# A perceiver layer on one core: queries of two tiles projected together, row normalisation moved to ScalarE, and self values moved behind values

## What is computed

```python
q = split_heads(layernorm(x) @ Wq.T + bq)          # 16 heads of 16
k = split_heads(ctx @ Wk.T + bk);  v = split_heads(ctx @ Wv.T + bv)
x = x + merge(softmax(q @ k.T) @ v) @ Wo.T + bo
x = x + self_attention(layernorm(x))               # RMS norm, rotary, sigmoid weights, 32 x 32 per batch
x = x + experts(layernorm(x))                      # 8 experts, top 1, capacity 160
```

## Time and profile before

| | us |
|---|---|
| three runs | 1109.96, 1110.98, 1110.84 (median 1110.84) |
| profiled execution, its own time | 1106.06 |
| its span, first to last instruction | 1104.1 |
| PE busy | 1066.6 (97%) |
| DVE busy | 882.3 (80%) |
| ACT busy | 796.4 (72%) |
| POOL busy | 244.1 (22%) |

### The profile page before, as it was taken

How to read it: one execution, slowest core, us unless ns; L and a number is a source line. 1 busy time by engine, 2 the same in 40 slices (tenths; PEclk the granted TensorE clock), 3 DMA queues, 4 the chain that set the end, 5 groups by cost and what they waited for, 6 DMA issues and landing times.

```text
span 1104.1 us, 40835 instructions
## 1 busy us (share of the span) xinstructions
PE 1066.6 (97%) x16195; PEld 869.6 (79%) x16195; DVE 882.3 (80%) x2652; ACT 796.4 (72%) x2319; POOL 244.1 (22%) x521
## 2 busy tenths in 40 slices
PE   6899999999999999999999999999999999988996
PEld 5678787787888788887787888788888778766996
DVE  6788798898888888888898888888888888874211
ACT  5778687788787787787787787787787787742221
POOL 1011212222222222212222222222222222221112
PEclk9999999999999999999999999999999999999998
DMA  7333422222221222112222221222212221001673
GB/s 202 109 101 102 154 63 67 68 68 64 60 64 44 61 62 57 49 50 60 61 61 61 60 60 42 59 56 56 48 48 58 58 61 36 17 12 47 207 249 110
DMA packets 69260, 82.04 MB, mean 74 GB/s; under 512 B 14331, under 2 KB 48076, under 8 KB 69072
## 3 DMA queue, kind: packets, MB, share of 16 engines
q1 hardware_dynamic: 64896, 75.06, 23.6%
q0 software_dynamic: 3360, 3.72, 1.0%
q10 hardware_dynamic: 816, 0.66, 0.2%
HBM read 64.79 MB, written 16.56 MB: 74 GB/s over the span
## 4 chain that ended last, share of the span: by engine, by line
PE 72%; DVE 18%; issue 4%; DMA 2%; ACT 1%; SPq 1%; POOL 1%; POOLq 0%; DVEq 0%; ACTq 0%
PE kps L416 12%; PE vps L428 12%; PE score L462 9%; PE score L448 5%; PE gather L477 5%; PE shared L486 5%; PE shared L501 4%; DVE prob L1092 4%; DVE nmx L1081 4%; PE score L778 3%; PE score L764 3%; PE shared L527 3%; DVE ctx_p L1073 2%; PE shared L405 2%; DVE th L1175 2%
## 5 line engine op out<-in xcount | busy, mean ns | idle before, releaser
L830 ACT ACTIVATE prob<-score,nmx 128x257 f32<-128x257 f32 x512 | 235.8, 475 | 95.8 <-DVE nmx L1081 95.8
L416 PE MATMUL kps<-ctx_p,wk_p 128*128 128x512 f32 x768 | 217.4, 411 | 0.0
L428 PE MATMUL vps<-wv_p,ctx_p 128*128 128x256 f32 x1536 | 215.5, 290 | 0.0
L1081 DVE TENSOR_REDUCE nmx<-score 128x2 f32<-128x514 f32 x256 | 165.2, 687 | 59.2 <-PE score L448 59.0
L428 PEld LDWEIGHTS vps<-wv_p,ctx_p 128*128 128x128 f32 x1536 | 191.7, 190 | 14.1 <-issue 12.7
L416 PEld LDWEIGHTS kps<-ctx_p,wk_p 128*128 128x128 f32 x768 | 138.1, 190 | 38.5 <-issue 13.6
L1092 DVE TENSOR_SCALAR prob<-prob,rsum 128x256 f32<-128x256 f32 x512 | 159.3, 354 | 9.1
L462 PE MATMUL score<-const,prob 128*128 128x128 f32 x1024 | 153.5, 278 | 5.5 <-DVE prob L1092 3.3
L1558 POOL TENSOR_TENSOR rstd<-ve,const 128x1 f32<-128x1 f32 x64 | 53.2, 831 | 464.6 <-DVE ve L1210 235.7
L462 PEld LDWEIGHTS score<-const,prob 128*128 128x128 f32 x1024 | 114.7, 141 | 16.3 <-DVE prob L1092 14.9
L847 ACT ACTIVATE ctx_p<-ctxT,nlast 128x256 fp32r<-128x256 f32 x256 | 116.0, 511 | 4.2 <-issue 4.2
(11 more groups left out here) (227 smaller groups left out, 1734.7 us busy)
## 6 DMA issues: line engine op xcount, KB each, us to landing
ctxT<-in_ctxT SPq DMA_DIRECT2D x128, 257.0 KB, 3.2
w<-in_w SPq DMA_DIRECT2D x16, 1024.0 KB, 8.1
xq<-in_x SPq DMA_DIRECT2D x32, 128.0 KB, 2.1
xr<-in_x SPq DMA_DIRECT2D x32, 128.0 KB
qbd<-qkT SPq DMA_DIRECT2D x248, 16.0 KB, 1.8
out<-row SPq DMA_DIRECT2D x31, 128.0 KB
slots<-row SPq DMA_DIRECT2D x10, 257.0 KB, 5.1
x_a<-slots SPq DMA_DIRECT2D x8, 129.0 KB, 2.1
```

What stands on the lines that cost most here:

```text
L416: last = mm(kps[:, :], wk_p[:, x, n, c * P:(c + 1) * P], ctx_p[:, y, n, 2 * r:2 * r + 2, :].rearrange("p j s -> p (j s)"), start=(n, x) == ...
L428: last = mm(vps[:, c, :], ctx_p[:, x, n, j, c * P:(c + 1) * P], wv_p[:, y, n, :], start=(n, x) == (0, LO), stop=(n, y) == (C - 1, LO))
L830: last = af(prob[:, m, :], score[:, m, 0:S], ACT.Exp, bias=nmx[:, m:m + 1], scale=1.0, accum_out=esum[:, m:m + 1])
L1081: v.tensor_reduce(nmx[:, 2 * c:2 * c + 2], score[:, 2 * c:2 * c + 2, 0:S], AX.X, ALU.max, negate=True).then_inc(s["max_done"], 1)
```

## The change

Seven edits go together.

1. The queries of tiles 1 to 30 are projected in 15 pairs. `project_pair` runs in every second pass, with fp32r parts of the weight (`wq_p`) and of the rows (`xnT_p`): 12 matmuls of 256 columns in place of twice 4 fp32 matmuls of 128 columns (which the profile counts as twice 8). Tiles 0 and 31 keep the old projection.
2. For the parts, ScalarE copies the high part of the transposed rows (`queries_hi`) and VectorE subtracts it (`queries_lo`, new in the sequence of j = 1). ScalarE's `queries` runs once per pair over 256 columns.
3. `norm_x_apply` moves from VectorE to ScalarE, behind the last copies of j = 3, for the tile three ahead; GpSimd computes the shift that it needs. `norm_x` moves ahead of `maxima(i, 3)`.
4. `sigmoid_product` moves behind `maxima(i, 1)`.
5. In j = 3 `norm2` moves between the two halves of `normalise`, and `context_lo(i + 1, 3)` behind `probsT(i, 3)`.
6. The first half of the self values moves from place (1, 1), ahead of the values, to (1, 2), behind them.
7. GpSimd waits for the normalisation of j = 1 before `rms`, and for that of j = 3 before `residual_bias2`.

In pass 0 the rows of tiles 1 and 2 are both normalised by VectorE and transposed, and SyncE waits for them before it loads the rows of tile 3.

```diff
+            def project_pair(p):
+                pe.wait_ge(s["xnT_parts"], 2 * p + 2)
+                if once(p):
+                    pe.wait_ge(s["wparts_done"], C + 2)
+                for c in range(C):
+                    for n in range(C):
+                        for x, y in PASSES:
+                            last = mm(shared[:, c * 2 * P:(c + 1) * 2 * P], wq_p[:, x, n, c * P:(c + 1) * P],
+                                      xnT_p[:, y, n].rearrange("p w q -> p (w q)"),
+                                      start=(n, x) == (0, LO), stop=(n, y) == (C - 1, LO))
+                last.then_inc(s["q_ps"], 1)
...
-                    (1, 1): s2 and (lambda: self_values(t2, range(0, 8))),
-                    (1, 2): lambda: (s1 and (spare_free(xa, i, 1), transpose_rows(y1, "y1_done", t1, "y1t_ps", spare_c)),
+                    (1, 2): lambda: (s2 and self_values(t2, range(0, 8)),
+                                     s1 and (spare_free(xa, i, 1), transpose_rows(y1, "y1_done", t1, "y1t_ps", spare_c)),
...
-                    (3, 1): q and (lambda: (turn("qT_done", i + 2), project_queries(i + 1))),
+                    (3, 1): q and half == 0 and (lambda: (turn("qT_done", queries_ready(i + 1)),
+                                                          project_pair(i // 2) if paired_tile(i + 1) else project_queries(i + 1))),
...
+            def norm_x_apply(t):
+                act.wait_ge(s["xn_shift"], t - 2)
+                act.wait_ge(s["qt_ps"], t)
+                af(xn[:, :], xq[:, :], ACT.Identity, bias=shift_q[:, 0:1], scale=rstd["q"][:, 0:1]).then_inc(s["xn_done"], 1)
...
+            def queries_lo(t):
+                dve.wait_ge(s["xnT_done"], t + 1)
+                w = (t - 1) % 2
+                v.tensor_tensor(xnT_p[:, LO, :, w, :], sh_c, xnT_p[:, HI, :, w, :].bitcast(F32), ALU.subtract
+                                ).then_inc(s["xnT_parts"], 1)
...
                 if xa:
                     normalise(i, 0)
-                if q and not once(i):
-                    norm_x_apply(i + 1)
                 if xa:
                     probsT(i, 0)
...
+                if xa:
+                    maxima(i, 1)
+                if once(i):
+                    queries_lo(1)
+                elif paired_tile(i + 2):
+                    queries_lo(i + 2)
                 if s2:
                     sigmoid_product(t2)
-
-                if xa:
-                    maxima(i, 1)
...
                 if once(i):
+                    norm_x(2)
+                    norm_x_apply(2)
                     setup_constants()
...
+                    if xa:
+                        pool.wait_ge(s["norm_done"], 2 * (TB * i + 2))
                     rms(t1)
...
+                    if xa:
+                        pool.wait_ge(s["norm_done"], 2 * TB * (i + 1))
                     residual_bias2(t1)
```

More of the change, by code:

```diff
@@ L448, in scores @@
                         last = mm(score[64 * e:64 * e + 64, m, 0:S],
-                                  qz[rows, half, e, j, :, :].rearrange("p h q -> p (h q)"),
+                                  qz[rows, buffer_of(t), e, j, :, :].rearrange("p h q -> p (h q)"),
                                   kT[rows, j // 2, e, j % 2, :], start=True, stop=True)
@@ L567, in turn, with next_queries @@
                 reader[bank] = sem_name, count
+            def next_queries(t):
+                turn(*(("xnT_parts", t) if paired_tile(t) else ("xnT_done", t + 1)))
+                transpose_queries(t)
             def spare_free(xa, t, j, c=0):
@@ L909, in _ @@
             act.wait_ge(s["bq_done"], 2)
-            queries(0, 0)
+            queries(0)
             act.wait_ge(s["wkv_in"], 16 * 5)
@@ L925, in body @@
                         gate_exp(t2 - 1)
-                    if j == 1 and q:
-                        copy_rows(xnT[:, :, :], sh_c, "qt_ps", i + 1, "xnT_done")
+                    if j == 1 and i <= T - 3:
+                        queries_hi(1 if once(i) else i + 2)
+                    if j == 2 and once(i):
+                        queries_hi(2)
                     if j == 3 and s1:
@@ L942, in body @@
                         squares(t1)
-                    if j == 3 and q:
-                        queries(i + 1, 1 - half)
+                    if j == 3 and q and half == 0:
+                        queries(i + 1)
                     if j == 3 and s2:
@@ L956, in body @@
                         sigmoid_exp(t2)
+                    if j == 3 and norms_ahead(i):
+                        norm_x_apply(i + 3)
                     if once(i) and j == 0:
                         context_hi(1, 0)
+                    if once(i) and j == 1:
+                        act.wait_ge(s["wq_in"], 16 * 4)
+                        weight_hi(wq_p[:, HI], wq[:, :, :])
                     if once(i) and j == 3:
@@ L1075, in context_lo, with maxima @@
                 last.then_inc(s["ctx_parts"], 1)
-            def maxima(t, j):
+            def queries_lo(t):
[3 more added lines that the diff above has]
+                                ).then_inc(s["xnT_parts"], 1)
+            def maxima(t, j, chunks=range(C)):
                 b = TB * t + j
-                for c in range(C):
+                for c in chunks:
                     dve.wait_ge(s["s_done"], 2 * b + c + 1)
@@ L1082, in maxima, with normalise @@
                                     ).then_inc(s["max_done"], 1)
-            def normalise(t, j):
+            def normalise(t, j, chunks=range(C)):
                 b = TB * t + j
-                for c in range(C):
+                for c in chunks:
                     dve.wait_ge(s["exp_done"], 2 * b + c + 1)
@@ L1340, in body @@
                 if xa:
-                    maxima(i, 2)
+                    maxima(i, 2, [0])
+                if once(i):
+                    queries_lo(2)
+                if xa:
+                    maxima(i, 2, [1])
                 if s1:
@@ L1623, in body @@
                     power("q", "xn_stat", 6, 1, "xn_pow")
+                    power("q", "xn_stat", 9, 2, "xn_pow")
                 if once(i, 1):
```

83 lines of the change are left out of this document (58 added, 25 removed).

## The result

The changed kernel takes 1127.46 us (median of 4 runs, 1126.56 to 1129.38), the kernel before 1110.40 on the same chip: ratio 1.0163, interval 1.0149 to 1.0178, 17.1 us slower.

What follows compares the result with a forecast made beforehand. VectorE's 5.85 us from residual to second normalisation in j = 1 was taken to hold up TensorE, which carries most of each pass. 9.2 - 1.5 + 1.4 + 2.0 = +11.1, giving 1121.9 us; range 1112 to 1130.

Steps and rivals of the forecast that it cites:

- the forecast's main step: VectorE's chain of j = 1: queries_lo enters it and costs 0.33 us in each of 28 passes, +9.2 us.
- the third rival: End of odd passes: GpSimd's residual_bias2 and residual_bias hold VectorE's moved context part, evac_v2 late; +7 us, 1129 us; 20%.
- Chain of j = 1: VectorE from residual to second normalisation: queries_lo makes TensorE wait 0.33 us longer in 28 passes, +9.2 us.
- Everywhere else in the pass VectorE waits for TensorE: Outside the chain of j = 1, VectorE waits for TensorE, such as 0.83 us ahead of the maxima of j = 3.
- Projection: Query projection on TensorE: 12 matmuls take 1.52 us instead of 1.62, saving 0.10 us in 15 pairs, -1.5 us.
- Odd passes ahead of `row`: Passes without a projection: TensorE reaches the row transposes before norm2 ends, 0.1 us in 14 passes, +1.4 us.
- `rms` and the slots, moves 0.4 us and has no reader for 3 us: GpSimd work queued behind its first new wait moves 0.4 us without a reader for 3 us; counted at nothing.
- needed only by keys of the next pass, 1 us later: The context part moved to the end of j = 3 is needed only by the next pass's keys; counted at nothing.
- Pass 0: First pass: norm_x(2) waits for tile 2's rows, so the maxima of j = 2 start 2.1 us late, +2.0 us.
- Self values: They only change places between L486 and the transposes, where TensorE waits at the stretch's end anyway; counted at nothing.

Runs made afterwards that it cites:

- E2: Kernel before plus one 128x256 VectorE tensor_scalar, to a tile nothing reads, behind the maxima of j = 1: 1116.23 us, ratio 1.0062.
- E5: Changed kernel with context_lo(i + 1, 1) moved behind weigh2, ahead of the maxima of j = 2: 1118.37 us, ratio 1.0081.
- E6: Kernel before with context_lo(i + 1, 1) moved behind weigh2: 1099.60 us, ratio 0.9912.
- E1: Changed kernel with context_lo(i + 1, 1) moved out of VectorE's chain of j = 1 to behind rows_lo: 1125.24 us, ratio 1.0144.
- E4: Changed kernel without GpSimd's new wait ahead of rms: 1123.84 us, ratio 1.0135.
- E3: Changed kernel with GpSimd's wait ahead of residual_bias2 put on evac_v2 of the same pass instead of the last normalisation: 1118.12 us, ratio 1.0079.
- E10: Changed kernel with the first half of the self values back ahead of the values: 1132.55 us, ratio 1.0216.
- E7: Changed kernel with the edits of E3, E4 and E5 together: 1114.51 us, ratio 1.0054.

## Why the prediction came out as it did

The time is 5.6 us above the forecast and inside the range: the forecast's main step and the third rival happened together. The steps, with sizes per stretch of the profiled execution:

- **Chain of j = 1, +9.2 forecast: right.** TensorE's wait there grew by 0.34 us (28 to 370 ns); the stretch from the keys to the end of the transposes, 5.11 us before and 5.41 after, by 0.30: 28 x 0.30 = 8.4. E2, E5 and E6 show it from three sides. The step "Everywhere else in the pass VectorE waits for TensorE" was too wide: put ahead of `att2n`, the context instructions make TensorE wait for that (E1).
- **Projection, -1.5: mis-sized.** A pair takes 1.403 us where two took 2 x 0.811, and the values behind it 1.438 instead of 1.518: 0.30 us a pair, -4.2 over 14. One matmul comes every 117 ns. That is nearer to the 109 ns that the formula of the Trainium skill (TensorE: Matmul & The Clock Gate, Back-to-back issue gap) gives as an estimate than to the 127 ns of the row that I preferred; the page says of its formula that it leaves out the weight loads, which each of these matmuls has.
- **Odd passes ahead of `row`, +1.4: mis-sized the other way.** From the values to the row transposes it is 1.84 us where 1.52 stood: 0.32 x 14 = +4.5. The power is not the reason: I let it fall half way to 0.55 us, and over the odd passes it took 0.63 on average (0.68 in the pass shown). Two other terms were too small: the transposes start 0.15 us behind the end of `norm2`, where I had allowed 0.04 for the hand-over, and the maxima of j = 3 start 0.08 us later behind their scores than before. In E4 the maxima are on time again, with `norm_x` still ahead of them, and 0.12 of the 0.32 us are gone, about half of what lies above the forecast; that half is the step "`rms` and the slots, moves 0.4 us and has no reader for 3 us": a GpSimd instruction costs by what it holds up, not only by who reads it. That this term and the projection miss by nearly as much, +3.1 and -2.7 us, and cancel is luck.
- **The third rival, 20%: it happened.** 0.98 - 0.62 = 0.36 us in 14 odd passes, +5.0; I had priced 0.5. The step that failed is "needed only by keys of the next pass, 1 us later": nothing waits for the context part, but `evac_v2` stands behind it. E3 undoes it with one line.
- **Pass 0, +2.0: +3.0.** The maxima of j = 2 start 15.9 us behind those of j = 0 (34.65 and 18.75), before 14.0 (31.52 in the earlier trace rows, and 17.53): +1.9, from the waits for `xq` and the power as forecast; 1.1 us more come behind them, up to the first `wo`.
- **Self values, at nothing: right in the sum,** but not for the reason given: their new place covers a late `th`. Back in the old place they cost 7 us, although the pauses are gone with it (E10).
- **Not foreseen: the pauses,** 4.0 against 0.5 us.

In the 26 stretches: 7.8 + 0.3 (the projection and `row`) + 4.6 + 3.5, and -1.6 from the keys behind the scores of j = 0, which run 0.06 us shorter, is 14.6; measured, 14.2.

What stays open: the 4 us of E3 that its profile does not show, the 2 us of E2's even passes, what the longer executions of E7 lost, and how the pauses depend on the order of the small matmuls.

## What to carry to other kernels

In these kernels an instruction on an engine that another one waits for was paid in full where it stood ahead of the last result that is waited for in that stretch; so list all such results (here `prob` and `att2n`) before choosing a place, and put what nobody needs behind the last of them: in the kernel before, moving two instructions there gave 0.9%. A move "into idle time" is to be weighed against what stands behind it on its own engine, and against what the other of VectorE and GpSimd does at that moment. Where an edit empties a wait, look at what was hidden behind it: late operands (`th`) and late instructions came out here.

## What the runs showed of the hardware

- A VectorE instruction with two SBUF inputs was held by GpSimd's tensor-tensor: 0.48 us alone, up to 0.88 beside `xr`, which had started 0.14 us earlier. The Trainium skill (SBUF — State Buffer, Who interferes with whom) says that the two exclude each other and that the first to start keeps the other out. The trace agrees that VectorE is held, by 0.40 us, while `xr` ran on for 0.60 us behind its start.
- A VectorE tensor-scalar from SBUF to SBUF, 0.35 us, took up to 0.61 beside GpSimd's indirect transfer instruction of 1.11 us, and never more than 0.36 when that instruction came sooner (E4).
- In small matmuls that follow each other every 10 to 40 ns TensorE made pauses of 0.26 to 1.04 us without a wait that the profile names (E7), each ending 1.2 to 1.6 us behind a packet of the instruction queue. That it had run out of instructions fits this and is not shown.
